# A quantised FFN behind a long convolution: the weight front loaded and ordered anew

## The chip, the cores and the metric

One core of a Trainium2 chip. The metric is device time in microseconds (us) of one execution. Engines: PE (TensorE), DVE (VectorE), ACT (ScalarE), POOL (GpSimd) and SP (SyncE, which here only issues DMAs); ACT and POOL issue DMAs too.

## The reference, cut to what matters

```python
# x: (64, 32, 512) f32; w_gate, w_up: (1376, 512); w_down: (512, 1376)
K = 2 * Re(einsum('hn,hnl->hl', Cs, exp(dtA * arange(512))))  # 32 heads, 64 complex modes
u = x * mask(length)                                  # one length per batch row
y = (causal_conv(u, K) + u * D) * mask(length)        # written with an FFT of length 1024
xq = int4_quant(y)                                    # per row: mean |y|, round, clip to -8..7
# bitlinear(a, w): w_q = clip(round(w / (mean|w| + 1e-5)), -1, 1); a @ (w_q * mean|w| * scale).T
g = square(relu(bitlinear(xq, w_gate, s_gate)))
inter = int8_quant(bitlinear(xq, w_up, s_up) * g)     # per row: max
out = x + bitlinear(inter, w_down, s_down)
```

## The kernel before, in words

The 64 x 32 rows are 16 tiles of 128: tile `n` holds heads `n` and `n + 16` of all 64 batch rows. There is no scheduler: each engine runs a list written out by hand, and semaphores tie the lists together.

**The front** (before the first matmul of tile 0's FFN, `products(0, 0)`, L609) does three things side by side.

1. Convolution kernel K. DVE computes 32-column exponentials and sines (L843 to L976), then powers (`raise_powers`, L297) and left factors (`left_factors`, L308) for the first four head pairs; this is called the tables here and ends with `early_tables` (L991). PE's `k_sums(0)` (L570) sums over modes, DVE's `k_copy(0)` (L1017) moves the result out, SP's `store_k(0)` (L355) writes it to DRAM, and `load_toep(n)` (L362) reads it back as a Toeplitz tile `toep` for `conv(n)` (L527). POOL makes the tables of the other heads (L474 to L484).
2. Ternary weights. A float matrix of 1376 x 512 is loaded into `raw[m]` (m = 0 gate, 1 up) by `load_inner` (L328); ACT sums |w| per part with `weight_sum` (L704); PE's `mean(m)` (L508) averages over partitions; DVE's `weight_mean(m)` (L978) makes the reciprocal `winv`; `weight_round` (L714 on ACT, L993 on DVE) writes rounded int16; PE's `turn(i)` (L552) transposes two blocks of 128 rows with eight matmuls (12 turns, order `TURNS`); `weight_copy(i)` (L729 ACT, L999 DVE) clips to -1..1 and leaves PSUM.
3. The first tiles: `xt(n)` transposes x (L518), `xt_copy(n)` on ACT (L734), `conv(n)` into PSUM, `y_mask(n)` on DVE (L1024), `y_sum`, `y_scale`, `y_round`, the transposed quantised row by `first_q(n)` on PE for n = 0, 1 (by an SP transposing DMA, `turn_q`, L373, from n = 2), and `q_copy(n)` (L1037).

In the kernel before, partition `p` of `raw[m]` holds rows `10p` to `10p+9` of the weight, and the last 96 rows lie in an eleventh block. So a partition reads 12 KB (blocks 0 to 5, part 0, `SPLIT = 6`, on SP's queue) or 8 KB (blocks 6 to 9, part 1, on ACT's queue) in one run. The two tails of 96 rows are on POOL's queue (L430). The columns of the inner dimension stand permuted by this, and `down_round` (L720 ACT, L1004 DVE) permutes `w_down` alike by reading it with a step of ten.

**The loop** over m = 0 to 15 (L672 on PE, L774 on ACT, L1093 on DVE, L391 on SP): `products(m, 0..2)` are gate and up matmuls over 416, 512 and 448 columns, ACT does `relu_square(c)`, DVE `gated(c)`, a row maximum and the rounding into `inter_q` (L1144), SP transposes `inter_q` by DMA (L395), PE does `down` from m = 5 on, and `conv(m + 4)` and `xt(m + 4)` keep four tiles ahead. w_down is loaded from POOL's queue (L492), its mean is taken in tile m = 2 (`mean(2)`, `weight_mean(2)`), its four 128-row blocks are rounded in m = 2 (two on DVE, two on ACT), transposed by SP's `turn_down` (L378) in m = 2 and 3 and copied in m = 4. `inter_q` has one buffer: DVE waits before L1144 until the transposing DMA of the tile before has landed.

Two matmuls of 512 columns into a scratch bank, `keep_clock(n)` (L566), stand before `conv(0)`, and four behind `k_sums(0)`.

Of the kernel before, what the change touches and what calls it, by code (L numbers as in the profile page):

```python
# [5 lines left out]
P = 128  # L6
# [17 lines left out]
def adaln_ffn(nc, x, length, log_dt, C, log_A_real, A_imag, Dskip,  # L24
# [16 lines left out]
    SPLIT = 6  # L41
# [14 lines left out]
    with ExitStack() as ctx:  # L56
# [19 lines left out]
        TURNS = (0, 1, 6, 7, 2, 8, 3, 9, 4, 10, 5, 11)  # L76
        TURN_BANK = (0, 1, 2, 3, 0, 1, 2, 3, 1, 3, 1, 3)
        COPY_ACT, COPY_DVE = (2, 3, 4, 8, 10, 11), (0, 1, 5, 6, 7, 9)
# [75 lines left out]
        wsum = sb("wsum", [P, 3, 2])  # L154
# [43 lines left out]
        w_loaded = [[sem(f"w_loaded{m}{i}") for i in range(2)] for m in range(3)]  # L198
        tail_loaded = [sem(f"tail_loaded{m}") for m in range(2)]
# [23 lines left out]
        w_rounded = [[sem(f"w_rounded{m}{i}") for i in range(2)] for m in range(3)]  # L223
# [39 lines left out]
        def weight_part(m, i):  # L263
            if m == 2:
                return (slice(None), slice(None), slice(0, IT_HALF) if i == 0 else slice(IT_HALF, I))
            cut = SPLIT
            return (slice(None), slice(0, cut) if i == 0 else slice(cut, None), slice(None))
# [77 lines left out]
        def _(sp):  # L345
# [74 lines left out]
        def _(pool):  # L420
# [9 lines left out]
            for m, w in enumerate((w_gate, w_up)):  # L430
                pool.dma_start(raw[m][0:IR, WIDE, :], w[WIDE * P:I, :]).then_inc(tail_loaded[m], 16)
# [42 lines left out]
            for i, (h0, h1) in enumerate(K_PARTS[1:]):  # L474
# [6 lines left out]
                if i == 0:  # L481
                    for j in range(2):
                        pool.wait_ge(w_rounded[1][j], 1)
                    load_quad(pool, 1)  # L484

            pool.wait_ge(toep_loaded[0], 32)
            for i in range(2):
                pool.wait_ge(w_rounded[0][i], 1)
            down_rows = w_down.rearrange("(c p) i -> p c i", p=P)
            for i in range(2):  # L490
                s = weight_part(2, i)
                pool.dma_start(raw[2][s], down_rows[s]).then_inc(w_loaded[2][i], 16)  # L492
# [7 lines left out]
        def _(pe):  # L500
# [7 lines left out]
            def mean(m):  # L508
                pe.wait_ge(w_summed, 2 * m + 2)
# [3 lines left out]
                for i in range(2):  # L513
                    mm = pe.matmul(down_ps[:, m:m + 1], averaging[:], wsum[:, m, i:i + 1],  # L514
                                   start=(i == 0), stop=(i == 1))
                mm.then_inc(w_mean_ps, 1)

            def xt(n):  # L518
                pe.wait_ge(x_loaded[n // 4], 32)
                wait(pe, xt_copied, n)  # L520
                if n == EARLY:
                    pe.wait_ge(q_copied, 2)
# [29 lines left out]
            def turn(i):  # L552
                m, g = TURNS[i] // IG, TURNS[i] % IG
                pe.wait_ge(w_rounded[m][0 if 2 * g + 2 <= SPLIT else 1], 1)
# [32 lines left out]
            turn(0)  # L587
            turn(1)
            xt(1)
            turn(2)  # L590
            turn(3)
            keep_clock(2)
            conv(0)
            turn(4)
            turn(5)
            xt(2)
            conv(1)
            k_sums(1)
            turn(6)
            turn(7)  # L600
            turn(8)
            xt(3)
            first_q(0)
            turn(9)
            conv(2)
            turn(10)
            turn(11)
# [64 lines left out]
            for m in range(T):  # L672
                products(m, 0)
                if m == 0:
                    first_q(1)
                products(m, 1)
                if m == 0:
                    conv(3)
# [4 lines left out]
                if m + EARLY < T:  # L683
# [510 lines left out]
```

## Time and profile before

| | us |
|---|---|
| median of 3 runs | 219.95 (219.66 to 222.68) |
| the profiled execution | 222.14 |
| its span, first to last instruction | 220.3 |
| PE / DVE / ACT / POOL busy in the span | 179.0 / 159.1 / 116.6 / 36.7 |
| mean granted TensorE clock | 0.985 |

The profiled execution's own time lies 1.8 us above its span and 2.2 us above the median. Times in the trace are us from the start of the span. A row of the timeline is: start, duration, engine with line, operation, written tile <- read tiles, shape, count, and in brackets the idle time before it with what ended it. SPq, ACTq and POOLq rows are issues of DMAs.

### The profile page before, as it was taken

To read this page: it belongs to the slowest core of one execution; us is meant where nothing else is said; L and a number is where in the kernel's file an instruction comes from. 1 tells how busy PE (TensorE), PEld (TensorE's weight loads), DVE (VectorE), ACT (ScalarE), POOL (GpSimd) and SP (SyncE) were. 2 spreads that over 40 slices of the span, in tenths; PEclk is the share of its full clock that TensorE was granted. 3 is DMA by queue.
4 is the path that set the end of the run, shared out by engine and by line. 5 is a ranking of instruction groups with operands and counts; after the bars stand their busy time and mean duration, and the time that the engine had idled before them with its cause. 6 is when DMAs were issued, how large, how long until landed. Compare 5 with 4: busy or idle time off the path is not lost.

```text
span 220.3 us, 3351 instructions
## 1 busy us (share of the span) xinstructions
PE 179.0 (81%) x1085; PEld 93.6 (43%) x1085; DVE 159.1 (72%) x424; ACT 116.6 (53%) x189; POOL 36.7 (17%) x88
## 2 busy tenths in 40 slices
PE   1005169969898895975999999999999999999983
PEld 1004066744463442432545454454545444444442
DVE  6996244555677798269986877878796978889662
ACT  2054567448767999044638182644628174450820
POOL 8534923991000052000000000000000000000000
PEclk9999999999999999697999999999999999999999
DMA  5999493728956589999335556473545254471624
GB/s 162 389 323 282 78 299 100 172 95 290 272 139 109 105 197 194 236 295 192 69 119 116 148 110 167 117 159 121 115 119 119 58 101 87 101 148 40 133 51 95
DMA packets 45439, 34.25 MB, mean 156 GB/s; under 512 B 37102, under 2 KB 37390, under 8 KB 44782
## 3 DMA queue, kind: packets, MB, share of 16 engines
q1 hardware_dynamic: 43070, 24.93, 49.2%
q0 software_dynamic: 1760, 6.36, 10.6%
q10 hardware_dynamic: 592, 2.75, 3.8%
q8 instruction: 9, 0.15, 0.3%
q14 instruction: 8, 0.07, 0.1%
HBM read 21.07 MB, written 4.28 MB: 115 GB/s over the span
## 4 chain that ended last, share of the span: by engine, by line
PE 71%; DMA 10%; ACT 9%; issue 5%; DVE 3%; SPq 1%; ACTq 0%
PE gate_ps L619 16%; PE up_ps L624 13%; PE down_ps L656 11%; DMA raw<-in_L_ffn_w_up_dram 10%; PE conv_ps L538 8%; PE tr_dve_ps L538 6%; PE conv_ps L656 4%; PE down_ps L538 3%; PE tr_act_ps L524 3%; ACT g L780 2%; ACT int L723 2%; PE up_ps L562 2%; ACT x_t L737 2%; ACT int L711 1%; PE gate_ps L562 1%
## 5 line engine op out<-in xcount | busy, mean ns | idle before, releaser
L780 ACT ACTIVATE g<-gate_ps,gu_scale 128x416 f32<-128x416 f32 (+2 forms) x48 | 30.5, 635 | 62.2 <-PE gate_ps L619 62.2
L1099 DVE SCALAR_TENSOR_TENSOR inter<-up_ps,gu_scale,g 128x416 f32<-128x416 f32 (+2 forms) x48 | 33.3, 694 | 23.5 <-ACT g L783 21.6
L624 PE MATMUL up_ps<-up_t,q_t 128*128 128x416 bf16 (+2 forms) x192 | 45.0, 357 | 1.8 <-DVE inter L1099 1.8
L619 PE MATMUL gate_ps<-gate_t,q_t 128*128 128x416 bf16 (+2 forms) x192 | 45.2, 358 | 0.1
L1103 DVE TENSOR_REDUCE imax<-inter 128x1 f32<-128x416 f32 (+2 forms) x48 | 30.3, 631 | 1.7
L783 ACT ACTIVATE g<-g 128x416 f32<-128x416 f32 (+2 forms) x48 | 28.1, 586 | 1.5
L656 PE MATMUL down_ps<-down_t,i_t 128*128 128x512 bf16 (+1 forms) x121 | 27.9, 379 | 0.0
L624 PEld LDWEIGHTS up_ps<-up_t,q_t 128*128 128x128 bf16 x192 | 18.6, 98 | 20.7 <-DVE inter L1099 2.7
L619 PEld LDWEIGHTS gate_ps<-gate_t,q_t 128*128 128x128 bf16 x192 | 17.6, 98 | 15.9 <-issue 2.7
L538 PE MATMUL conv_ps<-toep,x_t 128*64 128x512 f32 (+3 forms) x128 | 20.5, 467 | 4.5 <-ACT x_t L737 4.5
L711 ACT ACTIVATE int<-raw 128x2560 bf16<-128x2560 f32 (+2 forms) x6 | 15.2, 2530 | 14.4 <-issue 7.6
L514 PE MATMUL down_ps<-wsum,averaging 128*128 128x1 f32 x12 | 2.5, 314 | 20.8 <-ACT int L711 20.8
L656 PEld LDWEIGHTS down_ps<-down_t,i_t 128*128 128x128 bf16 (+1 forms) x121 | 11.8, 98 | 13.7
L538 PEld LDWEIGHTS conv_ps<-toep,x_t 128*64 128x64 f32 x128 | 9.0, 144 | 17.1 <-issue 9.7
L538 PE MATMUL tr_dve_ps<-toep,x_t 128*64 128x512 f32 (+3 forms) x80 | 13.6, 488 | 2.4 <-ACT x_t L737 2.4
L1144 DVE TENSOR_SCALAR inter_q<-inter,iscale 128x1376 int16<-128x1376 f32 x15 | 14.0, 936 | 0.5
L749 ACT ACTIVATE y_int<-y,yscale 128x512 int16<-128x512 f32 x16 | 11.5, 721 | 3.3 <-DVE yscale L1035 3.2
L514 PEld LDWEIGHTS down_ps<-wsum,averaging 128*128 128x128 f32 x12 | 2.5, 279 | 21.9 <-ACT int L711 21.8
L338 POOL DMA_DIRECT2D raw<-in_x_dram x6 | 5.6, 935 | 37.0 <-DVE winv L982 26.4
L538 PEld LDWEIGHTS tr_dve_ps<-toep,x_t 128*64 128x64 f32 x80 | 5.9, 150 | 11.0 <-issue 7.5
L737 ACT COPY x_t<-tr_act_ps 128x512 f32<-128x512 f32 x16 | 9.1, 571 | 2.1 <-PE tr_act_ps L524 2.1
L656 PE MATMUL conv_ps<-down_t,i_t 128*128 128x512 bf16 (+1 forms) x44 | 10.2, 379 | 0.0
(183 smaller groups left out, 227.4 us busy)
## 6 DMA issues: line engine op xcount, KB each, us to landing
toep<-k_back SPq DMA_DIRECT2D x16, 512.0 KB, 3.9
out_dram<-o_sb SPq DMA_DIRECT2D x30, 128.0 KB, 2.4
raw<-in_x_dram POOLq DMA_DIRECT2D x6, 512.0 KB, 7.8
raw<-in_L_ffn_w_gate_dram SPq DMA_DIRECT2D x1, 1536.0 KB, 14.0
raw<-in_L_ffn_w_up_dram SPq DMA_DIRECT2D x1, 1536.0 KB, 21.7
raw<-in_L_ffn_w_down_dram POOLq DMA_DIRECT2D x1, 1472.0 KB, 10.8
raw<-in_L_ffn_w_down_dram POOLq DMA_DIRECT2D x1, 1280.0 KB, 7.7
raw<-in_L_ffn_w_gate_dram ACTq DMA_DIRECT2D x1, 1024.0 KB, 5.5
```

The source lines that it names most:

```text
L538: mm = pe.matmul(bank[half * B:(half + 1) * B, 0:L - i * P], x_t[n % 2][:, i, half * B:(half + 1) * B], toep[n % 4][:, half, i * P:L], sta ...
L619: mm = pe.matmul(gate_ps[bank][:, 0:cn], q_t[m % 3][:, i, :], gate_t[:, i, c0:c0 + cn], start=(i == 0), stop=(i == KB - 1))
L624: mm = pe.matmul(up_ps[bank][:, 0:cn], q_t[m % 3][:, i, :], up_t[:, i, c0:c0 + cn], start=(i == 0), stop=(i == KB - 1))
L656: mm = pe.matmul(bank[:], i_t[n % 2][0:r, c, :], down_t[0:r, c, :], start=(c == 0), stop=(c == IB - 1))
L711: nc.scalar.activation(w_bits[m][weight_part(m, i)], raw[m][weight_part(m, i)], ACT.Abs, accum_out=wsum[:, m, i:i + 1]).then_inc(w_summed, 1)
L737: nc.scalar.copy(x_t[n % 2][:].rearrange("p k t -> p (k t)"), tr_act_ps[:]).then_inc(xt_copied, 1)
L749: nc.scalar.activation(y_int[n % 2][:], y[n % 3][:], ACT.Copy, scale=yscale[n % 2][:]).then_inc(y_rounded, 1)
L780: nc.scalar.activation(g2[bank][:, 0:cn], gate_ps[bank][:, 0:cn], ACT.Relu, scale=gu_scale[m % 4][:, 0:1]).then_inc(relu_done, 1)
L783: nc.scalar.activation(g2[bank][:, 0:cn], g2[bank][:, 0:cn], ACT.Square).then_inc(g2_ready, 1)
L1099: v.scalar_tensor_tensor(out=inter[:, c0:c0 + cn], in0=up_ps[bank][:, 0:cn], scalar=gu_scale[m % 4][:, 1:2], in1=g2[bank][:, 0:cn], op0=AL ...
L1103: return v.tensor_reduce(imax[:, c:c + 1], inter[:, c0:c0 + cn], AX.X, ALU.max, apply_absolute_value=True)
L1144: v.tensor_scalar(inter_q[:, 0:I], inter[:], iscale[:], None, ALU.mult).then_inc(inter_quant, 1)
```

## The change

- `load_inner`: partition `p` of block `c` now holds row `128c + p`, so every read is a piece of 2 KB. Three parts (`PARTS`: blocks 0 to 3, 4 to 7, 8 to 10, the last with the 96 rows of the tail) instead of two. SP's queue: gate part 1, up part 0, up part 2, half of x. ACT's queue: gate parts 0 and 2, up part 1 (behind a wait on `dve_consts` and the table load), half of x. POOL issues no weights.
- ACT: three sums of gate in the order 0, 1, 2; then up's sum 0, gate's round 0, up's sums 1 and 2, gate's round 1. DVE rounds gate part 2 and all of up.
- PE: `turn(0)`, `turn(1)` stand ahead of `k_sums(0)`; six turns instead of four ahead of `conv(0)`; `keep_clock(4)` is gone; `conv(2)`, `xt(3)` move from the front into tile 0's `products`, where `conv(3)` and `conv(4)` already were.
- DVE: `weight_mean(0)` stands between the base values and the powers of the tables instead of behind them.
- w_down is issued from ACT's queue ahead of `y_sum(0)`, and `down_round` is one contiguous operation per block instead of a strided one and a rest.
- `q_copy(n)` for n >= 2: in tile n - 1 behind `gated(0)` instead of at the end of tile n - 2.
- `TURNS`, `TURN_BANK` and which engine copies which turn are changed to match.

```diff
-    SPLIT = 6
+    PARTS = [(0, 4), (4, 8), (8, IB)]
-        TURNS = (0, 1, 6, 7, 2, 8, 3, 9, 4, 10, 5, 11)
+        TURNS = (0, 1, 2, 6, 7, 3, 8, 9, 4, 10, 5, 11)
...
         def load_inner(eng, m, w, i):
-            full = w[0:WIDE * P, :].rearrange("(p c) k -> p c k", c=WIDE)
-            if i == 0:
-                eng.dma_start(raw[m][:, 0:SPLIT, :], full[:, 0:SPLIT, :]).then_inc(w_loaded[m][0], 16)
-            else:
-                eng.dma_start(raw[m][:, SPLIT:WIDE, :], full[:, SPLIT:, :]).then_inc(w_loaded[m][1], 16)
+            full = w[0:WIDE * P, :].rearrange("(c p) k -> p c k", p=P)
+            c0, c1 = PARTS[i]
+            eng.dma_start(raw[m][:, c0:min(c1, WIDE), :], full[:, c0:min(c1, WIDE), :]).then_inc(w_loaded[m][i], 16)
+            if c1 == IB:
+                eng.dma_start(raw[m][0:IR, WIDE, :], w[WIDE * P:I, :]).then_inc(w_loaded[m][i], 16)
...
@@ PE, the front
             mean(0)
+            pe.wait_ge(ident_ready, 1)
+            turn(0)
+            turn(1)
             pe.wait_ge(early_tables, 1)
             k_sums(0)
-            pe.wait_ge(ident_ready, 1)
-            keep_clock(4)
             mean(1)
             xt(0)
...
@@ PE, the loop
                 products(m, 0)
-                if m == 0:
-                    first_q(1)
                 products(m, 1)
                 if m == 0:
-                    conv(3)
+                    conv(2)
+                    first_q(1)
...
-                if m + EARLY < T:
+                if m > 0 and m + EARLY < T:
                     xt(m + EARLY)
                 products(m, 2)
+                if m == 0:
+                    xt(3)
+                    conv(3)
+                    xt(EARLY)
...
@@ ACT, tile 0
                 relu_square(2)
+                if m == 0:
+                    y_round(2)
+                    xt_copy(3)
                 if m + EARLY < T:
                     xt_copy(m + EARLY)
...
@@ DVE, ahead of the powers; the rounding of w_down; the loop
+            weight_mean(0)
             scratch_u, scratch_v = inter[:, 0:128], inter[:, 128:256]
...
-                v.tensor_scalar(w_int[2][:, k, 0:WIDE * P].rearrange("p (c t) -> p c t", t=P),
-                                raw[2][:, k, 0:WIDE * P].rearrange("p (t c) -> p c t", c=WIDE),
-                                winv[:, 2:3], None, ALU.mult)
-                v.tensor_scalar(w_int[2][:, k, WIDE * P:I], raw[2][:, k, WIDE * P:I], winv[:, 2:3], None,
+                v.tensor_scalar(w_int[2][:, k, 0:I], raw[2][:, k, :], winv[:, 2:3], None,
...
                 gated(0)
-                if m == 0:
-                    q_copy(1)
-                if m + 2 < T:
+                if 1 <= m < T - 1:
+                    q_copy(m + 1)
+                if 1 <= m < T - 2:
                     y_scale(m + 2)
...
-                if m + 2 < T and m + 2 >= 2:
-                    q_copy(m + 2)
```

PE's list in the front, before, from `mean(0)` to `keep_clock(2)` (L514 mean, L577 `k_sums`, L568 `keep_clock`, L524 `xt`, L562 `turn`, two turns to 16 matmuls):

```order
L514 MATMUL down_ps<-wsum,averaging 128x1 x2
L577 MATMUL tr_dve_ps<-pw,ka 40x32 x8
L568 MATMUL conv_ps<-steps,ident_bf 128x512 x4
L514 MATMUL down_ps<-wsum,averaging 128x1 x2
L524 MATMUL tr_act_ps<-ident,x_first 128x128 x4
L562 MATMUL up_ps<-ident_bf,int 128x128 x16
L524 MATMUL tr_act_ps<-ident,x_first 128x128 x4
L562 MATMUL gate_ps<-ident_bf,int 128x128 x16
L568 MATMUL conv_ps<-steps,ident_bf 128x512 x2
```

The same stretch now (L505 mean, L552 `turn`, L567 `k_sums`, L515 `xt`, L558 `keep_clock`):

```order
L505 MATMUL down_ps<-wsum,averaging 128x1 x3
L552 MATMUL up_ps<-ident_bf,int 128x128 x16
L567 MATMUL tr_dve_ps<-pw,ka 40x32 x8
L505 MATMUL down_ps<-wsum,averaging 128x1 x3
L515 MATMUL tr_act_ps<-ident,x_first 128x128 x4
L552 MATMUL up_ps<-ident_bf,int 128x128 x8
L552 MATMUL gate_ps<-ident_bf,int 128x128 x16
L515 MATMUL tr_act_ps<-ident,x_first 128x128 x4
L552 MATMUL up_ps<-ident_bf,int 128x128 x8
L558 MATMUL conv_ps<-steps,ident_bf 128x512 x2
```

Two turns now stand between the mean and the sums of K, and six turns in all stand ahead of the first convolution.

ACT's list from the loads to the first copy of x, before (L333 loads of weights, L338 of x, L711 sums, L717 a rounding):

```order
L333 DMA raw<-in_L_ffn_w_gate_dram 128x2048
L333 DMA raw<-in_L_ffn_w_up_dram 128x2048
L338 DMA x_first<-in_x_dram 64x2048
L753 ACT_TABLE_LOAD
L753 ACTIVATE warm<-averaging 128x1
L711 ACTIVATE int,wsum<-raw 128x2560
L711 ACTIVATE int,wsum<-raw 128x3072 x2
L711 ACTIVATE int,wsum<-raw 128x2560
L737 COPY x_t<-tr_act_ps 128x512
L717 ACTIVATE int<-raw,winv 128x2560
```

And now, from the last load of weights on (L699 sums, L705 roundings):

```order
L329 DMA raw<-in_L_ffn_w_up_dram 128x4x512
L336 DMA x_first<-in_x_dram 64x2048
L699 ACTIVATE int,wsum<-raw 128x2048 x2
L699 ACTIVATE int,wsum<-raw 128x1536
L699 ACTIVATE int,wsum<-raw 128x2048
L705 ACTIVATE int<-raw,winv 128x2048
L699 ACTIVATE int,wsum<-raw 128x2048
L699 ACTIVATE int,wsum<-raw 128x1536
L705 ACTIVATE int<-raw,winv 128x2048
L722 COPY x_t<-tr_act_ps 128x512
```

The rounding that `turn(0)` needs stands behind the sum of up's part 0, and the other sums of up behind it.

## Rows read from the trace of the kernel before

**Rows 1.** The chain that ended last: start, us, what; three pieces.
```profile
2.59 21.74 DMA raw<-in_L_ffn_w_up_dram
...
35.44 2.31 PE conv_ps L538 x16
...
60.75 0.81 PE gate_ps L619 x4
```
**Rows 2.** Busy by stretch (PE, PEld, DVE, ACT, POOL), then PEclk, DMA share, GB/s.
```profile
0.00:6.00 6.00, 0.68 (x5) 0.60 (x5) 4.22 (x18) 1.49 (x2) 5.36 (x15) 1.00 0.56 184
6.00:16.00 10.00, 0.00 (x0) 0.00 (x0) 9.42 (x72) 2.43 (x2) 4.55 (x14) 1.00 1.03 354
16.00:22.00 6.00, 2.91 (x22) 2.34 (x23) 3.80 (x20) 2.86 (x2) 2.52 (x12) 1.00 1.05 285
...
140.00:160.00 20.00, 20.00 (x114) 9.87 (x112) 15.89 (x37) 10.75 (x21) 0.00 (x0) 1.00 0.53 129
```
**Rows 3.** DMA queues from 8 to 11 us: q1 is SP's, q10 ACT's.
```profile
q1 hardware_dynamic: 46, 0.57, 55.1%
q10 hardware_dynamic: 42, 0.34, 32.4%
```
**Rows 4.** DMA issues of the page: KB, median us to landing; issued at 1.67.
```profile
raw<-in_L_ffn_w_gate_dram ACTq DMA_DIRECT2D x1, 1024.0 KB, 5.5
```
**Rows 5.** Timeline of ACT, front and tile 0.
```profile
16.18 2.76 ACT L711 ACTIVATE int<-raw 128x3072 bf16<-128x3072 f32 x1 [1.43 <-DMA raw<-in_L_ffn_w_gate_dram]
...
32.07 2.43 ACT L717 ACTIVATE int<-raw,winv 128x2560 int16<-128x2560 f32 x1
...
53.89 0.72 ACT L749 ACTIVATE y_int<-y,yscale 128x512 int16<-128x512 f32 x1 [0.21 <-DVE yscale L1035]
...
56.61 0.63 ACT L780 ACTIVATE g<-gate_ps,gu_scale 128x448 f32<-128x448 f32 x1 [2.00 <-PE gate_ps L619]
...
57.76 0.57 ACT L737 COPY x_t<-tr_act_ps 128x512 f32<-128x512 f32 x1
```
**Rows 6.** Timeline of DVE: first and last operation of the powers and factors.
```profile
13.90 0.18 DVE L302 TENSOR_TENSOR inter<-pw 128x16 f32<-128x16 f32 x1
...
18.95 0.22 DVE L320 TENSOR_TENSOR ka<-inter 64x64 f32<-64x64 f32 x1
```
**Rows 7.** Timeline of PE: mean, sums of K, turns, the waits for ACT.
```profile
19.09 1.01 PE L514 MATMUL down_ps<-wsum,averaging 128*128 128x1 f32 x4 [14.30 <-ACT int L711]
20.03 1.27 PE L577 MATMUL tr_dve_ps<-pw,ka 128*40 128x32 f32 x16
...
31.34 1.91 PE L562 MATMUL up_ps<-ident_bf,int 128*128 128x128 bf16 x16
...
37.67 1.07 PE L562 MATMUL up_ps<-ident_bf,int 128*128 128x128 bf16 x16
...
45.82 0.38 PE L548 MATMUL tr_act_ps<-ident_bf,y_int 128*128 128x128 bf16 x4 [1.85 <-ACT x_t L737]
...
58.38 2.38 PE L538 MATMUL conv_ps<-toep,x_t 128*64 128x512 f32 x16 [1.05 <-ACT x_t L737]
```
**Rows 8.** SP's issues, and landing times of the first five `toep`.
```profile
42.43 0.30 SPq L359 DMA_DIRECT2D k_back<-k_sb  x1
44.72 0.36 SPq L365 DMA_DIRECT2D toep<-k_back  x1
...
DMA to landing us min/median/max: 3.3/5.5/7.2
```
**Rows 9.** Timeline of DVE, tiles 2 and 3: rounding w_down, rounding a tile, the wait.
```profile
76.94 1.39 DVE L1006 TENSOR_SCALAR int<-raw,winv 128x1280 int16<-128x1280 f32 x1
...
81.96 0.94 DVE L1144 TENSOR_SCALAR inter_q<-inter,iscale 128x1376 int16<-128x1376 f32 x1
...
95.59 0.16 DVE L1143 RECIPROCAL iscale<-gam 128x1 f32<-128x1 f32 x1 [6.05 <-DMA raw<-inter_q]
```
**Rows 10.** Timeline of PE: a convolution in tile 3.
```profile
88.20 4.07 PE L538 MATMUL tr_dve_ps<-toep,x_t 128*64 128x512 f32 x16 [2.44 <-ACT x_t L737]
```

More of the change, by code:

```diff
@@ L197, in adaln_ffn @@
         rest_loaded = sem("rest_loaded")
-        w_loaded = [[sem(f"w_loaded{m}{i}") for i in range(2)] for m in range(3)]
-        tail_loaded = [sem(f"tail_loaded{m}") for m in range(2)]
+        w_loaded = [[sem(f"w_loaded{m}{i}") for i in range(3)] for m in range(3)]
         x_loaded = [sem(f"x_loaded{q}") for q in range(QUADS)]
@@ L222, in adaln_ffn @@
         winv_ready = sem("winv_ready")
-        w_rounded = [[sem(f"w_rounded{m}{i}") for i in range(2)] for m in range(3)]
+        w_rounded = [[sem(f"w_rounded{m}{i}") for i in range(3)] for m in range(3)]
         w_turned = sem("w_turned")
@@ L481, in _ @@
                 if i == 0:
-                    for j in range(2):
+                    for j in range(3):
                         pool.wait_ge(w_rounded[1][j], 1)
                     load_quad(pool, 1)
[L486 to L492, printed above, removed]
             pool.wait_ge(winv_ready, 3)
@@ L512, in mean @@
                     pe.wait_ge(y_masked, EARLY + 2)
-                for i in range(2):
+                for i in range(parts):
                     mm = pe.matmul(down_ps[:, m:m + 1], averaging[:], wsum[:, m, i:i + 1],
-                                   start=(i == 0), stop=(i == 1))
+                                   start=(i == 0), stop=(i == parts - 1))
                 mm.then_inc(w_mean_ps, 1)
@@ L580, in _ @@
             mean(0)
+            pe.wait_ge(ident_ready, 1)
+            turn(0)
+            turn(1)
             pe.wait_ge(early_tables, 1)
             k_sums(0)
-            pe.wait_ge(ident_ready, 1)
-            keep_clock(4)
             mean(1)
             xt(0)
-            turn(0)
-            turn(1)
-            xt(1)
             turn(2)
             turn(3)
+            turn(4)
+            xt(1)
+            turn(5)
             keep_clock(2)
             conv(0)
[L594 to L598, printed above, removed]
             turn(6)
             turn(7)
-            turn(8)
-            xt(3)
+            conv(1)
             first_q(0)
[L604 to L607, printed above, removed]
+            for i in range(8, len(TURNS)):
+                turn(i)
+            k_sums(1)
+            xt(2)
             def products(m, c):
@@ L1060, in _ @@
                                         op0=ALU.mult, op1=ALU.mult))
-            weight_copy(5)
             y_mask(0)
-            k_copy(1)
             weight_copy(6)
+            weight_copy(7)
             y_scale(0)
-            weight_copy(7)
+            q_copy(0)
             y_mask(1)
-            q_copy(0)
+            weight_copy(8)
             weight_copy(9)
             y_scale(1)
-            y_mask(2)
+            weight_copy(11)
+            k_copy(1)
             def i_cast(n):
@@ L1116, in _ @@
                 if m == 0:
-                    y_mask(3)
+                    y_mask(2)
+                    q_copy(1)
+                    y_scale(2)
                 if m == LAG - 1:
```

89 lines of the change are left out of this document (46 added, 43 removed).

## The prediction

> **What bounds the kernel now.** I read the chain of waits first. It begins with the load of up's part 0, which lands at 24.33 us, reaches the first convolution at 35.44 and the first products of tile 1 at 60.75 [rows 1]. From there PE is the bound: in the stretch 140 to 160 it is busy 20.00 of 20 us [rows 2]. So the change can win in two places only: before 60.75, where PE waits for DMA, tables and ACT, and in tiles 2 to 4, where DVE idles 6.05 us for a transposing DMA [rows 9]. Busy shares say nothing here: PE's list has the same work in both kernels, but for one `keep_clock(4)` that stands in idle time. I compare the starts of `conv(0)` and of `products(1, 0)`, ahead of which both kernels have done the same turns, convolutions 0 to 4 and tile 0.
>
> **The load.** Second view: bytes by stretch. 184 GB/s for 6 us is 1.10 MB, 354 for 10 us brings 4.64 MB by 16 us, 285 for 6 us 6.35 MB by 22 [rows 2]. The total to be loaded is unchanged: 2.82 MB gate, 2.82 up, 1.05 x. What changes is who comes first. From 8 to 11 us SP's queue moved 46 pieces and ACT's 42, though 0.57 and 0.34 MB [rows 3]: the queues take turns piece by piece. Before, SP's 12 KB pieces got the larger share of bytes; now all pieces of weights are 2 KB, and both queues get the same.
>
> When is up's part 0 in? On SP's queue it stands behind gate's part 1: 1024 pieces of 2 KB. ACT's queue has 1440 in front of nothing: gate 0 and 2, up 1, half of x. Before, ACT's first part of 1.05 MB had landed 5.5 us after 1.67 [rows 4], at 7.2, when only some 1.5 MB had been moved by all (1.10 + 1.2 x 0.354): ACT had a head start of over 0.5 MB. If it keeps a full one (470 pieces), nearly all of gate, up 0, up 1 and ACT's x are moved when up 0 is complete, 5.47 MB with the parameters: 16 + 0.83 / 0.285 = 18.9 us. With no head start it is 2048 pieces, 4.22 MB: 6 + 3.12 / 0.354 = 14.8. I take the middle, 17.0: ACT is still issued 0.45 us ahead, but its pieces are now small. Landing comes later than the mean: before, all but SP's half of x, 6.19 MB, was moved at 16 + 1.55 / 0.285 = 21.4, and up 0 landed at 24.33, 2.9 us late. Bounds 0 and 2.9, taken 2.4, near the row. Up's part 0 lands at 19.4.
>
> In a sentence of its own: the Trainium skill, "DMA: Bandwidth & Descriptors", section "Issuing engines are not separate DMA queues", holds that issuing from several engines saves the sequencer's issue time only. By that rule the two queues give no byte sooner, and only order counts; the total by stretch is what I use for up's last part too, so the sum is unchanged, but the rule speaks against any gain from spreading as such.
>
> **From there to `conv(0)`.** ACT sums part 0 of up: 2048 columns at the 2.76 us of 3072 are 1.84. It then rounds gate's part 0: 2.43 x 2048 / 2560 = 1.94 [rows 5]. PE's two turns at the slow rate are 1.91 less an overlap of 0.2, 1.7; `k_sums(0)` 1.2 [rows 7]. `k_copy(0)` and hand-offs 0.5, storing K on an idle queue 44.72 - 42.43 = 2.3, the first `toep` 3.3 to landing [rows 8], hand-off 0.1. Sum 12.9, so `conv(0)` starts at 32.3, where it was at 35.44: -3.1. Note that `k_sums(0)`, at 20.03 before [rows 7], now starts at 24.9 or so, since it is queued behind the turns; the old store of K, however, stood in SP's queue behind the loads, the new one doesn't.
>
> Beside it: the mean inside the tables. Gate's 2.85 MB and what goes with it are moved by about 11.5 and landed by 13.9; part 1, a little earlier, is still being summed then, and part 2's sum takes 1.4: ACT is done at about 15.7. `mean(0)` with six matmuls instead of four 1.01 x 1.5 = 1.5 [rows 7]. DVE would be free at 13.9 [rows 6] and stands still until 17.2: all of the powers and factors are queued behind it. With 0.5 for the reciprocal and 19.17 - 13.90 = 5.3 for the tables [rows 6] they end at 23.0 instead of 19.2. That is 3.8 us given up, hidden by the turns with 1.9 us to spare. Up's mean comes 3.2 us (two sums) after the rounding of gate 0 and is out at about 28.4; DVE's rounding of up's part 0, turns 3, 4, 5 and `xt(1)` fit by 32. The removed `keep_clock(4)` stood in a gap. The new wait ahead of up's load on ACT is for a memset of the first us.
>
> **From `conv(0)` to `products(1, 0)`**: 25.3 us before. Two turns more stand ahead of `conv(0)`: -1.0 (16 transposes 1.07, less overlap) [rows 7]. PE waited 1.85 and 1.05 for ACT [rows 7]. Now it waits in tile 0 ahead of `conv(3)`: relu and square take 57.76 - 56.61 = 1.15, `y_round(2)` 0.72, `xt_copy(3)` 0.57 [rows 5], less 1.2 of up products and `xt(3)`, and `y_sum(2)` delays relu: 1.3 to 1.8; ahead of `conv(4)` 0.6 for one copy; and 0.9 for DVE's copies ahead of turns 10 and 11. Together 3.0 to 3.3 for 2.9. Net -0.7 (bounds -1.0 and +0.5). w_down, 2.8 MB, is now issued at some 34 us, beside x for tiles 4 to 7; `conv(4)` needs that x only past 50, so it is hidden; were it not, each us late would cost one.
>
> **Tiles 2 to 4.** `down_round` on DVE: 1.39 for 1280 strided columns becomes one operation like L1144's 0.94 for 1376 [rows 9], so the first transposing DMA of w_down leaves 0.45 earlier. ACT gains more (its strided operations), but what ends the stage is DVE's wait at 95.59 for the transposed `inter_q`, which stands on SP's queue behind two transposes of w_down. Everything won behind the start of these is swallowed there; what was won ahead of it stays. -0.45 (bounds 0 and -2). The later `q_copy` costs nothing and saves nothing in the loop, where PE bounds: its one short operation sits ahead of `y_scale` instead of behind, covered by ACT's idle time; at the end of tile 0 it takes a wait of DVE away that nothing waits for.
>
> **The sum.** -3.1 - 0.7 - 0.45 = -4.25. The profiled execution took 222.14, so 217.9 in those terms; its span 216.0. The median of the runs is 2.2 lower than the profiled one, and against it the forecast is 219.95 - 4.25 = 215.7.
>
> **The rivals.**
> *Early load, tables bound.* If the queues share evenly and land quickly, up's part 0 is there by 17 and the turns are done before the tables. Then `k_sums(0)` starts at 23.0 and `conv(0)` at 30.4: -5.0 - 0.7 - 0.45 gives 213.8. For it: pieces of equal size; against: ACT's head start before.
> *Late load.* Full head start and full lag: 21.8, `conv(0)` 34.7, 219.95 - 0.75 - 1.15 = 218.0. For it: both are what was measured, with larger pieces.
> *The clock.* The same 16 transposes took 1.91 us at 31.3 and 1.07 at 37.7 [rows 7], and a convolution 2.38 [rows 7] and, in tile 3 after a wait of 2.44, 4.07 [rows 10]. The granted clock's column reads 1.00 over the front, so the durations must tell. If the slow level (1.2 instead of 2.4 GHz) lasts through `conv(0)`, that is 1.7 for it and 0.8 for the turns and transposes: 218.2. For it: the filler of four matmuls is gone and the front's work lies in pieces with gaps. Against: work is dense from 26 us on. The Trainium skill, "TensorE: Matmul & The Clock Gate", Part 1, says that the granted clock follows how busy the array has been of late; by it, the removed filler and the idle stretch before 23 us speak against this change.
> *Slower: a fixed price per piece.* Six times as many pieces; if each costs time of its own, the front's load, all of it, drags. At 240 GB/s instead of 354 from 6 us on, with a full head start, 5.47 MB are moved at 24.2, part 0 lands at 26.6, `conv(0)` at 39.5: +4.1 - 1.15, 222.9. It turns slower than before when part 0 lands later than 23.7, that is below some 285 GB/s. For it: 285 is what the stretch from 16 on had even with large pieces. Against: nothing in the rate shows an effect of size.
>
> **Chances.** Forecast 0.40, with own range 214.5 to 217; early load 0.19; late load 0.21; clock 0.11; per-piece price 0.09. A measurement of this kernel tells about 2% (4.4 us, below 215.55) from no change. The early case and just over half of the forecast's lie beyond it: faster 0.42. Slower by over 2% only in the worse half of the last: 0.05. Range 212.6 to 219.8.
>
> **What would show it.** In the profile after: up's part 0 sum on ACT starts near 19.4 (it landed at 24.33 before); the tables end near 23; the first turn starts near 23.2; `k_sums(0)` near 24.9 with no wait for DVE; `conv(0)` near 32.3 and waiting for `toep`; `products(1, 0)` near 56.9; DVE's wait in tile 3 still there, ending near 91.3; 140 to 160 still all PE. Wrong it would be if `conv(0)` waits for anything but the chain through ACT's rounding of gate 0, if tile 0 has a wait over 2 us, or if the wait for the transposed `inter_q` changes by more than 1 us against the tiles before.

## The result, and the profile after

The changed kernel takes 236.10 us as the median of its four runs (233.82 to 239.86), the kernel before 220.32 beside it (219.66 to 222.68). Two of the four, 238.22 and 239.86, were disturbed and are left out of comparisons; the ratio of the others to before is 1.060, 95% interval 1.046 to 1.073. The forecast was 215.7: the change makes the kernel slower by about 6%, and the prediction went the wrong way.

The profiled execution took 233.82 us with a span of 231.9, where before had 220.3: 11.6 us more. The chain that ended last (start, us, what) says where:

```profile
2.59 22.16 DMA raw<-in_L_ffn_w_up_dram
...
28.67 3.37 ACT int L699 x4
32.04 0.04 issue
32.08 1.44 PE down_ps L505 x6
...
39.63 2.30 PE conv_ps L529 x16
```

Against [rows 1]: up's part 0 lands at 24.75 (2.59 + 22.16), where before it had landed at 24.33, and the first convolution starts at 39.6 instead of 35.44. The same view for tiles 2 to 4:

```profile
81.21 1.78 DVE int L1001 x2
83.00 0.69 SPq L382
83.69 0.04 issue
83.73 10.12 SPq L382
93.85 0.04 issue
93.89 11.93 DMA raw<-inter_q
...
105.91 0.17 DVE iscale L1137
...
111.89 4.53 PE conv_ps L529 x16
```

Twice the chain spends over 10 us on DMA matters, one behind the other. The second one of `turn_down` spends 10.12 us in SP's queue, and the transpose of tile 2's `inter_q` behind it takes 11.93. The timelines of DVE and PE show who waits for it, and what the stretches cost:

```profile
105.91 0.16 DVE L1137 RECIPROCAL iscale<-gam 128x1 f32<-128x1 f32 x1 [13.82 <-DMA raw<-inter_q]
```
```profile
108.32 1.68 PE L609 MATMUL up_ps<-up_t,q_t 128*128 128x448 bf16 x4 [9.50 <-DVE inter L1091]
111.89 4.53 PE L529 MATMUL conv_ps<-toep,x_t 128*64 128x512 f32 x16 [1.89 <-ACT x_t L722]
```

DVE's wait, 6.05 in [rows 9], is 13.82. PE idles 9.50, and its next convolution takes 4.53, where one at the fast level takes 2.38; before, the same convolution was slow too and took 3.92, and the one in [rows 10] 4.07. The granted clock of 100 to 120 us is 0.57 of the full 2.4 GHz, so for most of the stretch it stood at the lower level of 1.2; before it was 0.91 (busy by stretch, same columns as [rows 2]):

```profile
6.00:16.00 10.00, 0.00 (x0) 0.00 (x0) 7.50 (x60) 3.12 (x3) 3.57 (x12) 1.00 0.89 313
16.00:22.00 6.00, 1.44 (x6) 1.35 (x6) 1.84 (x15) 2.35 (x4) 0.02 (x1) 1.00 1.07 254
...
100.00:120.00 20.00, 9.74 (x35) 3.85 (x37) 12.62 (x26) 4.30 (x9) 0.00 (x0) 0.57 0.92 173
140.00:160.00 20.00, 19.90 (x112) 10.01 (x113) 16.04 (x38) 10.76 (x22) 0.00 (x0) 1.00 0.56 133
```

The loads move 313 and 254 GB/s where they moved 354 and 285; 140 to 160 is all PE in both. So the 11.6 us are two things. I read them with two marks that every kernel here has. M1 is the start of `products(1, 0)`, 60.7 before and 65.0 after: +4.3, the front. From M1 to the start of `products(6, 0)` (M6) it is 54.7 before and 62.0 after: +7.3, the stage in which w_down is turned. Behind M6 both run 9.87 us a tile. This is the split of two single executions: five other kernels with the same front, below, start conv(0) at 37.4 to 38.6, so that the front alone may cost anything from 2.0 to 4.2 us at conv(0).

### The profile page after: what moved, and what is told of

Same layout as the page of the kernel before. It is cut to its first block, busy times and chain, and to the rows that moved or that the text cites. A ratio compares the mean times of both kernels' runs of the same rounds, so it can differ in the third digit from the quotient of the medians.

```text
span 231.9 us, 3341 instructions
## 1 busy us (share of the span) xinstructions
PE 179.8 (78%) x1069; PEld 95.7 (41%) x1085; DVE 157.1 (68%) x424; ACT 116.1 (50%) x191; POOL 31.9 (14%) x84
## 4 chain that ended last, share of the span: by engine, by line
PE 63%; DMA 15%; DVE 6%; ACT 6%; SPq 5%; issue 4%; DVEq 0%; ACTq 0%
PE gate_ps L604 14%; PE up_ps L609 12%; PE down_ps L641 10%; DMA raw<-in_L_ffn_w_up_dram 10%; PE conv_ps L529 8%; DMA raw<-inter_q 5%; SPq L382 5%; PE conv_ps L641 4%; PE tr_dve_ps L529 4%; PE down_ps L529 3%; PE tr_act_ps L515 3%; ACT int L699 2%; PE gate_ps L552 1%; ACT g L768 1%; DVE inter L1091 1%
## 5 line engine op out<-in xcount | busy, mean ns | idle before, releaser
L768 ACT ACTIVATE g<-gate_ps,gu_scale 128x416 f32<-128x416 f32 (+2 forms) x48 | 30.3, 632 | 58.2 <-PE gate_ps L604 58.1
L609 PE MATMUL up_ps<-up_t,q_t 128*128 128x416 bf16 (+2 forms) x191 | 45.6, 362 | 9.6 <-DVE inter L1091 9.5
L1091 DVE SCALAR_TENSOR_TENSOR inter<-up_ps,gu_scale,g 128x416 f32<-128x416 f32 (+2 forms) x48 | 33.3, 693 | 24.6 <-ACT g L771 24.3
L604 PE MATMUL gate_ps<-gate_t,q_t 128*128 128x416 bf16 (+2 forms) x180 | 43.4, 361 | 0.6
L529 PE MATMUL conv_ps<-toep,x_t 128*64 128x512 f32 (+3 forms) x128 | 21.2, 477 | 3.6 <-ACT x_t L722 3.6
L699 ACT ACTIVATE int<-raw 128x2048 bf16<-128x2048 f32 (+3 forms) x8 | 15.6, 1944 | 14.6 <-DMA raw<-in_L_ffn_w_gate_dram 8.2
L641 PEld LDWEIGHTS down_ps<-down_t,i_t 128*128 128x128 bf16 (+1 forms) x121 | 11.8, 98 | 13.7
L529 PEld LDWEIGHTS conv_ps<-toep,x_t 128*64 128x64 f32 x128 | 9.1, 147 | 17.4 <-issue 11.3
L505 PE MATMUL down_ps<-wsum,averaging 128*128 128x1 f32 x16 | 3.4, 324 | 13.8 <-ACT int L699 13.8
L726 ACT ACTIVATE y_abs<-y 128x512 bf16<-128x512 f32 x16 | 9.9, 616 | 7.0 <-DVE y L1019 7.0
L529 PE MATMUL tr_dve_ps<-toep,x_t 128*64 128x512 f32 (+3 forms) x80 | 11.9, 439 | 1.4 <-ACT x_t L722 1.4
L552 PE MATMUL up_ps<-ident_bf,int 128*128 128x128 bf16 (+1 forms) x44 | 4.9, 285 | 10.0 <-ACT int L705 9.0
L1137 DVE RECIPROCAL iscale<-gam 128x1 f32<-128x1 f32 x15 | 2.5, 163 | 14.3 <-DMA raw<-inter_q 13.8
## 6 DMA issues: line engine op xcount, KB each, us to landing
raw<-in_x_dram POOLq DMA_DIRECT2D x6, 512.0 KB, 13.8
```

Of the source, the lines that this page charges most:

```text
L529: mm = pe.matmul(bank[half * B:(half + 1) * B, 0:L - i * P], x_t[n % 2][:, i, half * B:(half + 1) * B], toep[n % 4][:, half, i * P:L], sta ...
L604: mm = pe.matmul(gate_ps[bank][:, 0:cn], q_t[m % 3][:, i, :], gate_t[:, i, c0:c0 + cn], start=(i == 0), stop=(i == KB - 1))
L609: mm = pe.matmul(up_ps[bank][:, 0:cn], q_t[m % 3][:, i, :], up_t[:, i, c0:c0 + cn], start=(i == 0), stop=(i == KB - 1))
L641: mm = pe.matmul(bank[:], i_t[n % 2][0:r, c, :], down_t[0:r, c, :], start=(c == 0), stop=(c == IB - 1))
L699: nc.scalar.activation(w_bits[m][weight_part(m, i)], raw[m][weight_part(m, i)], ACT.Abs, accum_out=wsum[:, m, i:i + 1]).then_inc(w_summed, 1)
L768: nc.scalar.activation(g2[bank][:, 0:cn], gate_ps[bank][:, 0:cn], ACT.Relu, scale=gu_scale[m % 4][:, 0:1]).then_inc(relu_done, 1)
```

## Experiments

Two questions were asked: why are transposes slow in tiles 2 to 4, and why is up's part 0 late? A quad is the x of four tiles. In the edits, `load_quad(pool, q)` is one of x's late quads of 1.05 MB; `it_loaded[2]` and `down_turned[3]` are the transposes' semaphores. Theory J holds that x's loads slow the transposes that run beside them, because x's pieces take turns with the transposes' packets of some 250 bytes (0.17 MB in 691). All numbers of place (M1, M6, starts, waits) come from one profiled execution each; those of a_x2early (224.39 us) and a_order (235.79) were the longest of their kernel. The table has them together; "part 0" is the start of ACT's sum of up's part 0, "wait" DVE's longest for the transposed `inter_q`.

| kernel | part 0 | conv(0) | M1 | M1 to M6 | wait | median us | ratio to before |
|---|---|---|---|---|---|---|---|
| before | | 35.4 | 60.7 | 54.7 | 6.1 | 220.3 | |
| after | 24.8 | 39.6 | 65.0 | 62.0 | 13.8 | 236.1 | 1.060 (1.046 to 1.073) |
| a_x3late | 24.3 | 37.4 | 62.7 | 58.1 | 6.4 | 230.1 | 1.034 (1.020 to 1.047) |
| a_x2early | 23.9 | 37.5 | 67.4 | 50.2 | 3.2 | 222.2 | 0.989 (0.970 to 1.007) |
| a_x23 | 23.7 | 38.6 | 66.5 | 50.2 | none | 225.0 | 1.009 (1.003 to 1.016) |
| b_x23 | | 35.5 | 60.8 | 50.8 | none | 219.6 | 0.986 (0.972 to 0.999) |
| a_bigpieces | 17.4 | 33.9 | 61.1 | 65.1 | 18.5 | 234.0 | 1.050 (1.034 to 1.066) |
| a_smalllate | 22.1 | 36.0 | 61.3 | 65.5 | 18.3 | 233.8 | 1.049 (1.036 to 1.061) |
| a_xlast | 20.4 | 34.5 | 59.9 | 65.7 | 17.6 | 230.6 | 1.034 (1.013 to 1.056) |
| a_order | 24.1 | 37.8 | 63.1 | 65.9 | 19.2 | 233.5 | |
| a_stage | 23.3 | 37.7 | 63.1 | 50.6 | 4.9 (tile 0) | 219.7 | 0.983 (0.976 to 0.990) |
| a_all | 18.4 | 32.4 | 57.8 | 49.0 | 3.3 (tile 0) | 213.1 | 0.957 (0.951 to 0.964) |
| b_best | | 34.9 | 60.3 | 51.0 | none | 217.6 | 0.976 (0.971 to 0.981) |
| a_xsplit | 23.6 | 37.4 | 62.8 | 58.1 | 10.5 | 228.2 | 1.031 (1.012 to 1.049) |

Before was measured again beside each group: 223.98 us for the four of x, 222.42 for the four of the front, 222.56 for a_stage, a_all and b_best, 221.76 for a_xsplit. The ratios are to these, and medians of different groups are not to be set against each other. a_order's two runs (231.23 and 235.79) are too far apart for a ratio.

**x out of the stage, a_x3late and a_x2early.**

```diff
+            pool.wait_ge(it_loaded[2], 16)      # a_x3late
             load_quad(pool, 3)
```
```diff
                     load_quad(pool, 1)
+                    load_quad(pool, 2)           # a_x2early
...
-            pool.wait_ge(winv_ready, 3)
-            load_quad(pool, 2)
```

> Changed kernel, with the load of x for tiles 12 to 15 held until the transposing DMA of tile 2's row has landed. In the changed kernel that DMA (issued at 93.9, landed at 105.8) stood behind two transposes of w_down that shared the 16 DMA engines with 2.1 MB of x. Theory J (x's 4 KB packets take turns with the transposes' 256 B packets, so the transposes crawl while x is loading): with half of x gone from the jam the wait of DVE shrinks from 13.8 us to 6 to 9, total 228 to 230. Rival K (the transposes of w_down are slower for a reason of their own, such as the data or the layout): the wait stays above 12 us and the total within 1% of the changed kernel's, 232 to 236.

> Changed kernel, with x for tiles 8 to 11 loaded right behind x for tiles 4 to 7 (at about 41 us) instead of at 81. Theory J: again half of the competing x is gone from the stage at 82 to 105, DVE's wait shrinks to 6 to 9 us, total 227 to 230; the earlier load may push w_down's landing some 3 us later, which nothing waits for before 62. Rival K: wait above 12 us, total 232 to 236.

One quad out of the way takes DVE's wait from 13.8 to 6.4, the other to 3.2, and M1 to M6 by 3.9 and 11.8 us. Each move brings its own new collision. With quad 3 behind it(2) the turns of w_down's second half wait beside it (5.2 us for one). With quad 2 sent early, `toep(4)` is late, and `conv(4)` waits 3.8 us: M1 is at 67.4 though conv(0) is as in the others. The expectation did not foresee this.

**Both together, in after and in before, a_x23 and b_x23.**

> Changed kernel with both edits: no load of x beside the first transposes of w_down. Theory J: three transposes then take what they take alone (about 5 us each with their issue), DVE's wait is 0 to 3 us, total 222 to 225, so that only the 4.3 us lost in the front remain against the kernel before. Rival K: total above 230.

> Kernel before with both edits. Theory J: its wait of 6.05 us at 89.6 goes to nearly nothing, the clock does not fall in tiles 3 and 4, total 211 to 215. Rival K: no change, 219 to 221.

The wait for `inter_q` is gone in both. What is left of the stage in a_x23 is this chain:

```profile
92.56 3.87 SPq L382
96.42 0.04 issue
96.46 8.88 DMA int<-int
```

That is w_down's third or fourth turn beside quad 3, which now starts behind it(2). That x's loads are what slows the transposes is shown, and the rival, a cause in the transposes themselves, falls: SP spends 3.77 us on issuing the first pair of turns here, 11.68 in after. It holds in before too, whose stage loses 3.9 us of its 54.7; its ratio, 0.986, is near the edge of what can be told, and its median of 219.6 is far from the 211 to 215 expected. With x gone the two kernels' stages are alike, 50.2 and 50.8, so the +7.3 between M1 and M6 is what x costs: 11.8 us in after and 3.9 in before. Why x's pieces do so, the second half of theory J, is not shown by this.

**The front, four single changes.**

```diff
-  full = w[0:WIDE * P, :].rearrange("(c p) k -> p c k", p=P)
+  full = w[0:WIDE * P, :].rearrange("(p c) k -> p c k", c=WIDE)   # a_bigpieces
...
+  pool.wait_ge(w_loaded[0][1], 16)     # a_smalllate, ahead of POOL's small loads
...
-  load_half(act, 0, 1)                  # a_xlast: both halves of x last on SP
...
-  load_half(sp, 0, 0)
+  load_quad(sp, 0)
```

> The changed kernel with gate and up read in one run per partition ("(p c) k" where it has "(c p) k"): four inner rows lie side by side, so the pieces are 8 KB again, while the three parts, their queues and their order stay. It leaves out the matching order of w_down's columns, so its output is not the reference's. Theory P (the 2 KB pieces have a price of their own and make up's part 0 late): part 0 lands at 19 to 21 us instead of 24.78, the first convolution starts at 35 to 36.5 instead of 39.6, the program gains 3 to 4 us. Theory N (the rate is set by what else runs then, the small loads and x's pieces; size of the weight pieces is nothing): part 0 lands at 24 to 25, first convolution 39 to 40, no change of the whole beyond 1 us.

> The changed kernel with GpSimd's five first small loads (the tables of the rest) held until gate's part 1 has landed. Theory S (the fall of the rate at 9 to 11.5 us is these small pieces taking turns with the weights' pieces): gate's part 1 lands at 12.5 to 13.5 instead of 14.88, up's part 0 at 22 to 23 instead of 24.78, first convolution at 37 to 38. Theory N (they only coincide): gate's part 1 and up's part 0 stay within 0.5 us of 14.9 and 24.8.

> The changed kernel with both halves of the first x behind all weights on SP's queue; after has one of them on ACT's queue, where its 8 KB pieces start at about 17.5 us and take turns with up's part 0. Theory X (x's pieces slow the last part of up's part 0): part 0 lands at 22 to 23 instead of 24.78 and the first convolution, if x comes in time, starts at 37.5 to 38.5; x lands later, so that xt(0) may wait and take back up to 2 us. Theory N: part 0 stays at 24.3 to 25, since the bytes in flight from SP's queue only take x's place.

> The changed kernel with its order in the front put back in two places: the gate's mean behind the tables on VectorE (with the reading of the first turns), and k_sums(0) ahead of turn(0) and turn(1), k_copy(0) ahead of weight_copy(0). Tables then end at about 19.3 instead of 25.3, K is stored from about 23 instead of 32.3, and the toep load is hidden. Theory O (the stalled tables and the order of the turns set conv(0)): conv(0) starts at 35.5 to 37 instead of 39.6, since what is left is up's part 0 (24.78), its sum, its mean, its rounding and its turns. Theory U (the late up part 0 alone sets it): conv(0) starts at 38.5 to 39.6, because turn(5) of part 0 comes ahead of it in either kernel. The rounding of the gate waits on its mean: if that goes later than 20.2 us because the tables come first, gate rounding starts at 21 to 22, still ahead of up's sum end at 26.7.

Six kernels with after's front unchanged put the sum of part 0 at 23.3 to 24.8 and conv(0) at 37.4 to 39.6; that is the band against which one profile is to be read. Three of the four lie outside it.

a_smalllate: the queues between 9 and 12 us (packets, MB, share), of after and then with the small loads held:

```profile
q1 hardware_dynamic: 155, 0.32, 34.3%
q10 hardware_dynamic: 156, 0.27, 26.9%
q0 software_dynamic: 97, 0.00, 2.2%
```
```profile
q1 hardware_dynamic: 280, 0.55, 54.5%
q10 hardware_dynamic: 280, 0.51, 50.9%
```

In after the two queues move 311 pieces in these 3 us, 196 GB/s with all shares far below 100%, while q0 sends 97 tiny pieces; without them 560 pieces, 352 GB/s. The hole costs 0.47 MB, and gate's part 1 is summed from 12.82 instead of 14.88. The edit closes the hole, so the small loads are the cause. How they hold back engines that are idle by their own shares is not shown.

a_xlast: part 0 is there at 20.4, the largest step that needs no other layout. From 18 to 24 us after moves 1.32 MB (219 GB/s), 0.50 of it on ACT's queue and mostly x, beside up's 2 KB pieces on SP's; a_xlast moves 1.52 MB in that time, all but 0.03 from SP's queue, and up has come first.

a_bigpieces: ACT sums part 0 at 17.42 without waiting for it. The rate from 6 to 16 is 321 GB/s against 313, so 8 KB pieces move hardly faster while the hole is there (237 GB/s from 9 to 12, share 0.64). The share did it: from 6 to 12 us SP's queue, on which part 0 stands, moved 183 pieces and 1.37 MB against ACT's 180 and 0.60; in after it is 434 and 0.89 against 467 and 0.87. The counts are nearly equal in both, the bytes are not. ACT's queue was by then in gate's part 2, only two blocks wide, so that its runs are 4 KB, and 2 KB in the 96 rows of the tail. Theory P is right that the layout decides when part 0 lands; in this stretch it is by the queue's share and not by a price of each piece. From 16 to 22 us, though, the kernel moved 319 GB/s where after moved 254, and no run tells whether that is the pieces' size or what was left to load: a price of small pieces there stays open.

a_order: the tables come back to where they were, `k_sums(0)` starts at 19.73 instead of 30.61, and conv(0), at 37.8, stays within the band. It lies below the 38.5 to 39.6 of theory U and above the 35.5 to 37 of theory O. Since the band reaches down to 37.4 with tables and turns as in after, no cost of the stalled tables or of the order of the turns can be seen as long as part 0 is late, which is what theory U says.

None of the four kept what it gained at conv(0). a_bigpieces stands 5.7 us ahead of after at conv(0), 3.9 at M1 and 0.7 at M6; a_xlast 5.0, 5.1 and 1.4. DVE's wait grew from 13.8 to 17.6 to 19.2 in all four. The prediction said that what was won ahead of this stage stays, and it was swallowed as well. In all four, quad 2 is issued 1.03 us ahead of the first pair of turns and quad 3 3.80 us behind quad 2, just as in after, so why the jam is longer in them than in after no run shows.

**The stage mended, with and without the front, a_stage, a_all, b_best.**

```diff
+            pool.wait_ge(toep_loaded[0], 32)     # b_best: quad 2 right behind quad 1
             load_quad(pool, 2)
...
+            pool.wait_ge(down_turned[3], 16)     # all three
             load_quad(pool, 3)
```

In b_best quad 2 goes right behind quad 1, as in b_x23. a_all has a_smalllate's and a_xlast's edits and `k_sums(0)` ahead of the first two turns on top of a_stage.

> The changed kernel with x's late quads moved out of the stage of the transposes by two waits on POOL: quad 2 behind the landing of toep(4) (near 62 us, so that it doesn't delay that load as it did when it was sent right behind quad 1), quad 3 behind the landing of w_down's last transpose. Theory J (the jam in tiles 2 to 4 is x's pieces taking turns with the transposes'): no wait for it(2) of more than 2 us, no wait of more than 1 us for down_turned, products(6,0) about 8 us behind products(4,0)+11 rather than 23 as in after, total below before by 0 to 2 us (after minus 12 to 15). Rival M (quad 3 then comes too late for xt(12)): a wait of x_t at conv(12) of some us, and the total stays at or above before.

> a_stage with the three front remedies together: both x halves behind the weights on SP's queue, the small loads held until gate's part 1 has landed, k_sums(0) ahead of the first two turns. Each of the first two alone started conv(0) 3.6 to 5 us earlier and the whole gained nothing, since the wait for it(2) grew by as much. Theory W (that gain was swallowed by the jam, so with the jam gone it shows): conv(0) at 33 to 34.5, and the program 3 to 5 us below a_stage, 4 to 6 below before. Rival V (the front is covered by something else behind it, such as x_t, toep or w_down): less than 1.5 us below a_stage, with a new wait named by the profile between products(0,0) and products(4,0).

> The kernel before with x's quads moved alike: quad 2 right behind quad 1, quad 3 behind the landing of w_down's last transpose instead of it(2)'s. Theory J: the wait for it(2) of 6.05 us in before is gone and the one for down_turned of 0.3 us stays small; the program gains 4 to 6 us on before (ratio 0.973 to 0.982). Rival: quad 3 is late for xt(12), which takes back 1 us or more.

Quad 3 behind the last turn of w_down costs nothing at `xt(12)` in any of the three, so rival M falls, and so does the rival of b_best, whose ratio of 0.976 is what was expected. The turns' issue time on SP (timeline of a_all's SP) is 4.3 us where after had 11.68:

```profile
76.72 4.36 SPq L382 DMA_TRANSPOSE int<-int  x2
81.12 1.47 SPq L394 DMA_TRANSPOSE raw<-inter_q  x1
83.66 1.19 SPq L375 DMA_TRANSPOSE q_int<-y_int  x1
85.53 4.30 SPq L382 DMA_TRANSPOSE int<-int  x2
89.87 2.52 SPq L394 DMA_TRANSPOSE raw<-inter_q  x1
```

With the jam gone the front counts: a_all is 5.3 us ahead of a_stage at conv(0), 5.3 at M1 and 6.6 in the median. Theory W expected 3 to 5 and was low; V falls. a_stage itself came out where J put it but has a jam of its own, since quad 2, now at 57.95, meets tile 0's transpose:

```profile
59.00 17.95 DMA it_int<-inter_q
```

It is the same collision at another place: one quad, 1.05 MB, against one transpose, which takes 4.3 us with no x beside it (median of two in after, 58 to 78 us). It costs DVE a wait of 4.9 us there, and 3.3 in a_all, which has this edit too. b_best has one of its own: the transposed row of y takes 9.71 us to land, and DVE waits 3.6 for it.

a_all takes 213.09 us where before takes 222.56 beside it: 4.3% faster than before, and by the two ratios (0.957 / 1.060) some 10% faster than after. The change's front is worth having, once x is out of its way.

**Smaller pieces of x, a_xsplit.**

```diff
+            if q >= 2:
+                for h in range(4):
+                    eng.dma_start(dst[:, h, 0:L], x[:, h0 + h, :]).then_inc(x_loaded[q], 16)
+                return
...
-                pe.wait_ge(x_loaded[n // 4], 32)
+                pe.wait_ge(x_loaded[n // 4], 128 if n >= 8 else 32)
```

> The changed kernel with quads 2 and 3 of x loaded by one transfer per head instead of one per four heads: the same bytes at the same place in the program, in more and smaller pieces (4 KB in the records of after). Theory T (the queues take turns by piece, so what slows the transposes is that each of x's turns is long): with pieces of half the size the transposes get more of the time, the wait for it(2) falls from 13.8 us to 6 to 9, turn_down's issue from 11.7 to 7 to 9, and the program gains 4 to 7 us on after. Theory B (what slows them is x's bytes or its row pitch, whatever the size of a piece): wait and total stay within 2 us of after, or x's slower pieces make it worse. If the pieces stay at 4 KB in the records, the run says nothing on either.

x's 2.10 MB came in 768 pieces instead of 576, so a piece shrank from 3.6 to 2.7 KB, not by half. The wait is 10.5 (13.8), the turns' issue 4.29 and 9.10 (11.68 for one pair), M1 to M6 58.1 (62.0). The direction is that of theory T and the size is short of it; its issue is also spread, 9.4 us on POOL for what took 3.7. Theory T is supported, not settled: pieces of another size and a load spread over more time were changed together.

## Why the prediction was wrong

The sum was -3.1 - 0.7 - 0.45. Measured between the two profiles it is +4.2, +0.1 and +7.3.

**Step 1, the load (failed).** "Up's part 0 lands at 19.4". It landed at 24.75, in other profiles of the same front at 23.3 or later. Two terms of the sum failed. The byte count kept before's rates, 184, 354 and 285 GB/s in the three stretches, and they were 156, 313 and 254. And the middle between no head start of ACT's queue and a full one was wrong: up's part 1, on ACT's queue, had landed at some 21.7 (3.29 + 18.4), ahead of part 0, so the head start was full. With these two the prediction's own working gives 5.47 MB at 21.5, and with its lag of 2.4 to 2.9 a landing at 23.9 to 24.4. Two causes lay behind it that the sum had no term for. POOL no longer sent the weights' tails ahead of its small loads, so these came earlier (5.3 to 7.5 us from issue to landing, 15.5 to 18.0 before) and made a hole of 0.47 MB in the middle of the load. And the 1.05 MB of x had one half on ACT's queue beside the end of part 0. With both taken away, in a_all, part 0 is summed from 18.4 us, a little ahead of the forecast. That "all pieces of weights are 2 KB, and both queues get the same" was right, 501 pieces on q1 and 500 on q10 from 12 to 18 us, but x's pieces stayed at 8 KB: the turns read from [rows 3] were applied to the weights and not to x. The rival of the late load, with the full head start and part 0 at 21.8, was right on the head start and still too early, by the rates.

The rival with the price per piece gave conv(0) at 39.5, which is what one profile shows, but with part 0 at 26.6. The mechanism that it named is not what made the hole, since a_bigpieces has it as well and a_smalllate, with 2 KB pieces, moved 379 GB/s from 6 to 16 us. For 16 to 22 us it is open, as said.

The Trainium skill, "DMA: Bandwidth & Descriptors", section "Queues, rings and completion order", says that each DMA engine goes round the queues it has work for a packet at a time. The packets of the profile come about equally from both queues in the front, 434 to 467 and 183 to 180, and not where x meets the transposes, 258 to 691 (below). A packet in that section of the Trainium skill holds several descriptors, and whether those of the profile are the same thing no run shows, so this is neither for nor against it.

**Step 2, from part 0 to conv(0) (right, with the clock open).** Predicted 12.9 us. It is 13.1 in a_x3late (24.30 to 37.37, where the last wait is 0.70 for `toep`, as forecast), and 14.8 in after. Most of the difference is the clock. Here are the same 16 turns of gate in after, and in a_x3late:

```profile
35.36 1.89 PE L552 MATMUL gate_ps<-ident_bf,int 128*128 128x128 bf16 x16
37.04 1.06 PE L515 MATMUL tr_act_ps<-ident,x_first 128*128 128x128 f32 x4
```
```profile
34.28 1.07 PE L553 MATMUL gate_ps<-ident_bf,int 128*128 128x128 bf16 x16 [0.15 <-DVE int L992]
35.18 0.61 PE L516 MATMUL tr_act_ps<-ident,x_first 128*128 128x128 f32 x4
```

PE had stood for 8.98 us before the first turn in after and 8.21 in a_x3late; the durations fall back to the fast level at 39 us in the one and at 31.6 in the other, so this part of the rival on the clock was real in one execution and absent in the next. The column of the granted clock reads 1.00 in both. In after the chain therefore went through ACT's sums, the mean (1.44 us, where a_x3late has 0.83) and the turns, not through K and `toep`.

The tables' stall was priced as hidden. They ended at 25.3, 6.1 later than before (3.8 predicted), DVE waiting 6.07 us for the mean because gate's part 1 was late too; a_order, with the tables where they were before and conv(0) still in the band, agrees that it was hidden.

**Step 3, conv(0) to M1 (off by 0.8).** Predicted 0.7 less, measured 25.40 against 25.32 before. The waits came as forecast: 1.54 ahead of conv(3) (1.3 to 1.8), 0.68 ahead of conv(4) (0.6), 1.2 for DVE's copies (0.9). The gain of two turns moved ahead of conv(0) was not seen at M1. w_down was hidden, as said. What a late load costs at this place a_x2early shows, where conv(4) waited 3.8 us for `toep(4)` and M1 came 29.9 us behind conv(0) instead of 25.4.

**Step 4, tiles 2 to 4 (failed, and the dearest).** Predicted -0.45 with bounds 0 and -2; measured +7.3. What the sum had at nothing was x: its loads beside the transposes cost 3.9 us of this stage before (b_x23) and 11.8 now (a_x23). The duration was right: DVE's two rounds take 1.78 together, 0.9 each, and ACT's shrank as well, to 1.43 us each where they had 2.57 and 0.36 in two pieces. The step counted what the faster rounds give to the turns of w_down and not what else waits for them. POOL holds quad 3 back until w_down is rounded. With ACT's half faster it was issued 3.8 us behind quad 2, where before had 6.6. Here are POOL's two loads and SP's first pair of turns, before and then after:

```profile
76.87 3.07 POOL L338 DMA_DIRECT2D raw<-in_x_dram  x2 [26.39 <-DVE winv L982]
83.52 1.23 POOL L338 DMA_DIRECT2D raw<-in_x_dram  x2 [3.58 <-ACT int L726]
78.53 5.72 SPq L383 DMA_TRANSPOSE int<-int  x2
```
```profile
81.14 1.99 POOL L336 DMA_DIRECT2D raw<-in_x_dram  x2 [28.45 <-DVE winv L976]
84.94 1.72 POOL L336 DMA_DIRECT2D raw<-in_x_dram  x2 [1.80 <-ACT int L711]
82.17 11.68 SPq L382 DMA_TRANSPOSE int<-int  x2
```

Both quads now lay across the first turns and it(2). That the earlier quad 3 is what made the cost grow from 3.9 to 11.8 is argued from these rows and only in part shown: with quad 3 held back altogether (a_x3late) DVE's wait is 6.4, near before's 6.05, but the first pair still takes 9.26 us beside quad 2 alone, and the stage 58.1, 3.4 above before. No run puts only the old 6.6 us back between the quads. The queues of after from 92 to 100 us (packets, MB, share):

```profile
q0 software_dynamic: 258, 0.94, 71.8%
q1 hardware_dynamic: 691, 0.17, 30.0%
```

In after the transposes' queue gets 0.17 MB of its little packets through in 8 us, beside 0.94 MB of x. Before, x came at the same rate, 0.49 MB from 86 to 90 us, and q1, with no other load issued in these 4 us, still moved 1410 packets and 0.35 MB beside it. So x at this rate does not by itself fix what a transpose loses, and what else does is open. "Everything won behind the start of these is swallowed there; what was won ahead of it stays" was wrong in its second half: the four front kernels, 2 to 6 us earlier at conv(0), had it(2) only at 105 to 110 us, as after had it at 106. The sign of being wrong that the prediction gave for this step, the wait for the transposed `inter_q` changing by more than 1 us, is there: +7.8.

The chance of 0.05 for slower was too small for a change that starts 2.8 MB of loads at another time and shortens what releases two more.

## What to carry to other kernels

When an operation gets faster, list everything that waits for its semaphore, DMA issues above all, and ask what those transfers will then lie beside; here two rounds that were each 1.5 us shorter on ACT released 1.05 MB of x 2.8 us sooner behind the load ahead of it, in a stage in which x cost 11.8 us. Keep bulk loads of long pieces out of the time in which small-packet DMAs (transposes, tiny loads) stand on the path: hold them with a wait on the last of these, as a_all does with quad 3. Judge a change in the front by marks inside the program, not by the total, as long as a later stage waits on something of its own.

## What the hardware showed

A transposing DMA of one tile takes some 4 us alone, 11.9 beside two quads of x and, in a_stage, 17.95 beside one; in the run with x in smaller pieces, which also spread its issue, DVE's wait was 10.5 us for 13.8. Some 97 pieces of a few bytes in 3 us came with a loss of 0.47 MB of weights, 196 GB/s where 352 were reached without them, and holding them brought it back. And the same front on the same program had its turns at the slow level until 39 us in one execution and until 31.6 in another, with the granted clock's column at 1.00 in both: for the first matmuls of a program the durations are the better witness.
